# A fused AdaLN block: softmax slots in pairs, a look-ahead of 24 maxima, gating spread over tiles, division by block turns

## What is computed

```
x: (4, 2048, 256);  mod = silu(c) @ wmod -> sa, ca, ga, sb, cb, gb  per batch
h = layernorm(x) * (1 + ca) + sa
x = x + ga * FAVOR_attention(h)          # 16 heads of 16, 64 random features each, linear in T
h = layernorm(x) * (1 + cb) + sb
x = x + gb * FFN(h)
FFN(h): 4 experts, each a quarter (512) of the tokens, h normalised once more,
        expert e uses the first m = 256 >> e channels;
        q, k, v from xn[:, :m];  8 heads of 32 over all 2048 tokens
        attn = softmax(q k^T * scale);  out_e = (attn @ v)[:, :m] @ o_w[:m, :m].T + o_b[:m], + h
```

## Time and profile before

| | |
|---|---|
| Median of 3 runs | 1817.99 us (1814.53 to 1819.95) |
| Profiled execution | 1821.6 us, span 1819.5 us |
| PE busy | 1704.0 us (94%), 11538 products |
| DVE busy | 1397.6 us (77%) |
| ACT, POOL busy | 1101.9 us (61%), 1142.2 us (63%) |
| Maxima: product, reduction | 960 x 447 ns, 960 x 681 ns |
| Scores, exponentials | 960 x 406 ns, 960 x 601 ns |
| Values, denominators | 1920 x 608 ns, 960 x 592 ns (two records to a product) |
| Mean granted clock | 0.975 |

### The profile page before, as it was taken

The page is one execution under the profiler, slowest core; times in us unless marked ns, Lnnn a source line. Parts: engine busy times, 40 slices in busy tenths (PEclk is TensorE's granted clock), DMA queues, the critical chain, the costliest instruction groups (busy, mean ns, idle before and its releaser), DMA issues.

```text
span 1819.5 us, 31846 instructions
## 1 busy us (share of the span) xinstructions
PE 1704.0 (94%) x11538; PEld 973.2 (53%) x11538; DVE 1397.6 (77%) x2621; ACT 1101.9 (61%) x2066; POOL 1142.2 (63%) x1062
## 2 busy tenths in 40 slices
PE   6999999999799989999989998999988999899997
PEld 4775544444477554444357755444436765444443
DVE  5887877777588788777678878777758888777774
ACT  1885536666588544666658844465656875356664
POOL 2784358667678345766768724776685862477666
PEclk8999989999999999999999999999999999899999
DMA  5000350010200045001120005300111001620101
GB/s 182 2 2 1 128 159 10 18 44 4 90 2 2 1 154 133 16 12 45 35 59 2 1 23 180 85 19 10 44 59 36 2 2 50 191 54 11 41 13 47
DMA packets 56076, 89.55 MB, mean 49 GB/s; under 512 B 13288, under 2 KB 31976, under 8 KB 53100
## 3 DMA queue, kind: packets, MB, share of 16 engines
q1 hardware_dynamic: 54768, 87.45, 16.4%
q10 hardware_dynamic: 1152, 0.07, 0.0%
HBM read 49.29 MB, written 35.72 MB: 47 GB/s over the span
## 4 chain that ended last, share of the span: by engine, by line
PE 67%; DVE 13%; ACT 8%; POOL 5%; issue 3%; DMA 2%; SPq 2%; ACTq 0%; POOLq 0%; DVEq 0%
PE PS L1466 14%; PE PS L1651 13%; PE PS L1639 11%; PE PS L1664 6%; PE PS L1364 5%; PE PS L1372 3%; PE PS L1389 3%; PE PS L1399 3%; DVE MXP L1067 3%; ACT HT L639 2%; ACT HTR L642 2%; DVE STAT L960 2%; ACT PR L860 1%; DVE QKS L1136 1%; PE PS L1515 1%
## 5 line engine op out<-in xcount | busy, mean ns | idle before, releaser
L602 POOL TENSOR_TENSOR TS<-PR 128x1024 f32<-128x1024 f32 (+1 forms) x256 | 573.5, 2240 | 300.4 <-ACT PR L860 235.9
L1067 DVE TENSOR_REDUCE MXP<-PS 128x1 f32<-128x512 f32 x960 | 600.5, 681 | 178.3 <-PE PS L1466 177.5
L860 ACT ACTIVATE PR<-PS 128x512 f32<-128x512 f32 x960 | 503.1, 601 | 355.6 <-PE PS L1639 351.0
L1466 PE MATMUL PS<-KOP,QOP 96*128 96x512 f32 x960 | 418.4, 447 | 11.6 <-DVE MXP L1067 5.0
L1639 PE MATMUL PS<-QOP,KOP 97*128 97x512 f32 x960 | 376.9, 406 | 14.8 <-ACT PR L860 11.5
L1466 PEld LDWEIGHTS PS<-KOP,QOP 96*128 96x128 f32 x960 | 184.4, 193 | 277.4 <-DVE MXP L1067 216.2
L1651 PE MATMUL PS<-PR,V 128*32 128x512 f32 x1920 | 275.7, 608 | 0.0
L1639 PEld LDWEIGHTS PS<-QOP,KOP 97*128 97x128 f32 x960 | 180.5, 191 | 77.9 <-ACT PR L860 45.9
L1664 PE MATMUL PS<-TS,ones 128*32 128x512 f32 x960 | 133.1, 592 | 5.5 <-POOL TS L602 5.5
L522 POOL TENSOR_SCALAR PK<-XSK 128x1024 f32<-128x1024 f32 x64 | 67.2, 1050 | 98.4 <-ACT XSK L698 98.1
L1399 PE MATMUL PS<-PB,QKT 64*128 64x256 f32 x1536 | 126.5, 297 | 1.0 <-DVE VE L954 1.0
(11 more groups left out here) (153 smaller groups left out, 2629.1 us busy)
## 6 DMA issues: line engine op xcount, KB each, us to landing
KOP<-k_scr SPq DMA_DIRECT2D x84, 256.0 KB, 5.5
k_scr<-QKS SPq DMA_DIRECT2D x64, 256.0 KB, 2.9
QOP<-q_scr SPq DMA_DIRECT2D x180, 64.0 KB, 2.0
q_scr<-QKS SPq DMA_DIRECT2D x40, 256.0 KB, 3.0
X<-in_L_attn_x_dram SPq DMA_DIRECT2D x16, 512.0 KB, 4.7
out_dram<-X SPq DMA_DIRECT2D x12, 512.0 KB, 3.1
QOP<-MXT SPq DMA_DIRECT2D x224, 0.5 KB
KOP<-QKS SPq DMA_DIRECT2D x36, 64.0 KB, 2.0
```

The costliest lines, as they stand in the source:

```text
L602: g.tensor_tensor(sums(k)[:, 0:len(stage)], pair[:, :, 0], pair[:, :, 1], ALU.add).then_inc(S["psum_t"], 1)
L860: a.activation(PR[:, k % 2, w, q], bank(score_bank(p, n, w, q)), ACT.Exp).then_inc(S["ex"], 1)
L1067: v.tensor_reduce(MXP[:, u % 2, i, kc:kc + 1], bank(max_bank(p)), AX.X, ALU.max).then_inc(S["am_rd"], 1)
L1466: mm(bank(max_bank(p)), QOP[0:96, u % QS6, i * P:(i + 1) * P], KOP[0:96, h % KS6, kc * CH:(kc + 1) * CH], start=True, stop=True).then_inc( ...
```

## The change

- PE: slots 0 to 7 (stage 0) as before, with the values of slot 7 at their end; from slot 8 on slots go in pairs: three times a maximum and a score, five times a score and a maximum, then the denominators of the pair before, then the values of both slots; an output stands behind them.
- `LOOK` is 24: two more maxima stand before slot 0, and the stream ends with pair 26 (slots 52 and 53).
- DVE: eight maxima to a pair; the additions of a finished stage behind the fifth and the eighth maximum of the next stage's first pair. The division of a part is one call: 32x32 block turns of the whole row of `SUM` (512 columns), the reciprocal of one column in 32, a copy that spreads it over 32 columns, and turns back; the buffers lie in rows of `Hh` that are free by then, which the wait on `base` makes sure of.
- ACT: the upper values are copied before the first exponentials of the next stage, the upper sums behind those of its second slot.
- POOL: the gate products are three pieces at tiles 4, 5 and 6 (`GATE` = 4); the bias follows seven tiles behind (`LAG` = 7). DVE's residual waits for the tiles that it reads and not for all.

```diff
@@ -84,7 +84,7 @@
 
-    LOOK = 22
+    LOOK = 24
     stream = [(0, i, kc) for kc in expert for i in range(TPC)]
...
@@ -92,7 +92,7 @@
     PER_P = 17
-    LAG = 4
+    GATE, LAG = 4, 7
     SETUP_BANK = (0, 1, 7, 2, 6, 7, 0, 1)
...
@@ -177,6 +177,9 @@
         Hh = sb("Hh", [P, NT, D])
+
+        TURN = Hh[:, NT - TPC:NT - TPC + 2].rearrange("p t d -> p (t d)")
+        ONE = Hh[:, NT - 1, 0:CH // DH]
 
...
@@ -501,15 +504,15 @@
 
-            def gated_output(b):
-                if b == 0:
+            def gated_output(b, part):
+                if b == 0 and part == 0:
                     wait_all(pool, (S["mod_in"], 16), (S["setup_ok"], 1))
-                gate = MODB[:, bass.ds(b, 1), 0, :]
-                g.tensor_tensor(WoG[:], WoT[:], gate.broadcast_to([P, KD, D]), ALU.mult).then_inc(S["gated"], 1)
-                g.tensor_tensor(BOG[:], BO[:], gate.rearrange("p o d -> p (o d)"), ALU.mult).then_inc(S["gated"], 1)
+                gate = MODB[:, bass.ds(b, 1), 0, :].rearrange("p o d -> p (o d)")
+                dst, src = (BOG[:], BO[:]) if part == KD else (WoG[:, part], WoT[:, part])
+                g.tensor_tensor(dst, src, gate, ALU.mult).then_inc(S["gated"], 1)
 
             def with_bias(b, t):
-                wait_all(pool, (S["gated"], 2 * (b + 1)))
+                wait_all(pool, (S["gated"], (KD + 1) * (b + 1)))
                 g.tensor_tensor(X[:, t], X[:, t], BOG[:], ALU.add).then_inc(S["xb"], 1)
...
@@ -524,8 +527,8 @@
                         low_h(b, t + 2)
-                    if at == LAG:
-                        gated_output(b)
+                    if GATE <= at < GATE + KD + 1:
+                        gated_output(b, at - GATE)
                     if at >= LAG:
...
@@ -607,7 +610,7 @@
                             rows = min(width[z], P)
-                            wait_all(pool, (S["rcp"], TPC * (len(RECIPROCALS) * b + i + 1)))
+                            wait_all(pool, (S["rcp"], len(RECIPROCALS) * b + i + 1))
                             g.tensor_tensor(NUM[0:rows, z], NUM[0:rows, z], SUM[0:rows, z], ALU.mult
...
@@ -833,13 +836,17 @@
 
-                def upper_rows(p):
+                def upper_values(p):
 
...
                     a.activation(CS[0:rows, 0], PS[2 * DH:2 * DH + rows, 6, :], ACT.Copy).then_inc(S["cs_up"], 1)
+
+                def upper_sums(p):
+
+                    rows = acc_rows(p)
                     act.wait_ge(S["den2"], SLOTS // 2 * b + STEPS // 2 * (p + 1))
...
@@ -854,14 +861,17 @@
                         act.wait_ge(S["psum_t"], SLOTS * b + k - 1)
+                    if n == 0 and p > 0:
+                        upper_values(p - 1)
                     for w in range(len(stages[p])):
...
                                          ).then_inc(S["ex"], 1)
-                    if n == 0 and p > 0:
-                        upper_rows(p - 1)
-                upper_rows(len(stages) - 1)
+                    if n == 1 and p > 0:
+                        upper_sums(p - 1)
+                upper_values(len(stages) - 1)
+                upper_sums(len(stages) - 1)
 
...
@@ -1105,8 +1115,7 @@
                     g, two = NC * b + s, slice(s * TPC + 2 * h, s * TPC + 2 * h + 2)
-                    if s == 0 and h == 0:
-                        dve.wait_ge(S["xb"], NT * (b + 1))
+                    dve.wait_ge(S["xb"], NT * b + TPC * s + 2 * h + 2)
                     dve.wait_ge(S["yps"], 2 * g + h + 1)
...
@@ -1201,30 +1210,35 @@
                 maxima(MAXU, LOOK)
-                for k in range(SLOTS):
-                    p0 = LOOK + k * 4
-                    if k % STEPS == 1 and k > STEPS:
-                        p = k // STEPS - 1
-                        maxima(p0, p0 + 1)
+                for m in range(SLOTS // 2):
+                    p0 = LOOK + 8 * m
+                    if m % (STEPS // 2) == 0 and m > 0:
+                        p = 2 * m // STEPS - 1
+                        maxima(p0, p0 + 5)
                         finish(dve, v, b, p, 0)
-                        maxima(p0 + 1, p0 + 2)
+                        maxima(p0 + 5, p0 + 8)
                         finish(dve, v, b, p, 1)
-                        maxima(p0 + 2, p0 + 4)
                     else:
-                        maxima(p0, p0 + 4)
-                    for z, at in RECIPROCALS:
-                        if k in (at, at + 1):
-                            if k == at:
-                                dve.wait_ge(S["c_out"], len(stages) * b + len(stages) - 2)
-                            for q in (2 * (k - at), 2 * (k - at) + 1):
-                                divide_part(z, q).then_inc(S["rcp"], 1)
+                        maxima(p0, p0 + 8)
+                    for i, (z, at) in enumerate(RECIPROCALS):
+                        if 2 * m == at:
+                            dve.wait_ge(S["c_out"], len(stages) * b + len(stages) - 2)
+                            dve.wait_ge(S["base"], 2 * NC * (b + 1))
+                            if i > 0:
+                                dve.wait_ge(S["rcp"], len(RECIPROCALS) * b + i)
+                            sums_divided(z).then_inc(S["rcp"], 1)
                     for i, e in enumerate(results[:-1]):
-                        if k == OUT_SLOTS[e]:
+                        if 2 * m == OUT_SLOTS[e]:
                             result(b, i)
 
-            def divide_part(z, q):
-                part = SUM[0:min(width[z], P) if z < NC else P, z, q * P:(q + 1) * P]
-                return v.reciprocal(part, part)
+            def sums_divided(z):
+
+                rows = min(width[z], P) if z < NC else P
+                own(v.transpose(TURN[0:rows], SUM[0:rows, z]))
+                own(v.reciprocal(ONE[0:rows], TURN[0:rows].rearrange("p (n k) -> p n k", k=DH)[:, :, 0]))
+                own(v.tensor_copy(TURN[0:rows].rearrange("p (n k) -> p n k", k=DH),
+                                  ONE[0:rows].rearrange("p (n o) -> p n o", o=1).broadcast_to([rows, CH // DH, DH])))
+                return v.transpose(SUM[0:rows, z], TURN[0:rows])
 
...
@@ -1261,8 +1275,9 @@
                 dve.wait_ge(S["fin_n"], len(stages) * (b + 1))
+                dve.wait_ge(S["rcp"], len(RECIPROCALS) * (b + 1))
+                own(sums_divided(NC))
                 for q in range(TPC):
-                    own(divide_part(NC, q))
                     part = slice(q * P, (q + 1) * P)
...
@@ -1505,7 +1520,7 @@
                     if s == 0:
-                        pe.wait_ge(S["gated"], 2 * (b + 1))
+                        pe.wait_ge(S["gated"], (KD + 1) * (b + 1))
                         pe.wait_ge(S["phiq"], 2 * NT * (b + 1))
...
@@ -1677,20 +1692,35 @@
                 pe.wait_ge(S["q_lo"], NQ * (b + 1))
-                for k in range(SLOTS):
+                def score_of_pair(m, i):
+
+                    score(2 * m + i // 4, i % 4 // 2, i % 2)
+
+                for k in range(STEPS):
                     p0 = LOOK + 4 * k
...
                         maxima(p0 + i, p0 + i + 1)
-                        if k > 0 and i // 2 < len(stages[k // STEPS]):
-                            score(k, i // 2, i % 2)
+                        if k > 0 and i < 2:
+                            score(k, 0, i)
                     if k >= 1:
...
                         denominators(k // 2 - 1)
+                values(STEPS - 1)
+                for m in range(STEPS // 2, SLOTS // 2):
+                    p0 = LOOK + 8 * m
+                    for i in range(3):
+                        maxima(p0 + i, p0 + i + 1)
+                        score_of_pair(m, i)
+                    for i in range(3, 8):
+                        score_of_pair(m, i)
+                        maxima(p0 + i, p0 + i + 1)
+                    denominators(m - 1)
+                    values(2 * m)
+                    values(2 * m + 1)
                     for i, e in enumerate(results[:-1]):
-                        if k == OUT_SLOTS[e]:
+                        if 2 * m == OUT_SLOTS[e]:
                             output(i)
-                values(SLOTS - 1)
                 denominators(SLOTS // 2 - 1)
...
```

## The result

The kernel with the change takes 1797.18 us (median of five runs, 1795.75 to 1804.53), the one before 1817.8 beside it (1814.53 to 1819.95). The ratio is 0.9894, with a 95% interval of 0.9872 to 0.9915: 1.1% faster, and outside the 0.3% that can't be told from no change. The profiled execution took 1797.2 us, its span 1795.4; the sum in the prediction had 1797.8 for it. Of the medians 1794 was forecast: the change took off 20.6 us where 24 were expected.

What follows compares the result with a forecast made beforehand. PE's matrix work was taken to bound the slot loop. Terms 27.8 - 4.8 + 5.0 + 0.6 - 4.8 = 23.8 us took the profiled 1821.6 to 1797.8, and the median 1818.0 to 1794 us; 8-in-10 range 1780 to 1811.

Steps and rivals of the forecast that it cites:

- The pair: Long slot loop, slots in pairs: 6.99 us a pair becomes 6.87; with stage beginnings and batch end, 27.8 us gained.
- rival of a free pair: Long slot loop: the weights' early load takes up the waits, a pair takes 6.71 us, kernel 1779 us; chance 0.15.
- that of 7.07: Rival in the long slot loop: the rings of three bound, a pair takes 7.07 us, kernel 1812 us; chance 0.14.
- score 4's early ask: Inside a pair: score 4 asks for its bank just as it is freed, putting the next product at 1.84, not 1.745.
- The stage beginnings: Where a stage begins in the slot loop: waits of 0.4 three times and 0.9 twice, 3.0 us a batch, should go.
- The look-ahead: Before the slots: two more maxima in DVE's unbroken run, 1.2 us a batch, a cost of 4.8 us.
- Pairs 27 to 31: Batch end, pairs without maxima: 6.43 us each, 0.98 more with an output; POOL's last sum ends at 7.50.
- Gating: Tiles 4 to 6 on POOL: gating spread and bias lag 7 save 1.26 a batch, 5.0 us.
- Joints: Between batches: POOL waits for the first variance behind output 2, 1.6 us lost each, 4.8 us for three.
- The end: Kernel end: division by block turns saves 0.6 us, once.
- Turn: DVE's division: a block turn of 512 columns taken as 0.70 us; a rival had 3.39, kernel 1835 us, chance 0.05.
- The clock: Rival in front of the slots: middle batches lose the 2 us batch 0 loses, kernel 1798 or 1803 us; chance 0.10.

Runs made afterwards that it cites:

- e1_strict: Changed kernel with maximum and score strictly alternating through all eight of a pair; 1835.8 us, ratio 1.0092 to the kernel before.
- e11_four: Changed kernel with outputs in PE's wait and no division copy (1784.2 us), now four maximum-score then four score-maximum in pairs with maxima; 1784.82 us.
- e2_look22: Changed kernel with a look-ahead of 22 instead of 24, pairs kept; 1814.29 us, ratio 0.9969 to the kernel before.
- e0_after_again: The changed kernel run once more, unchanged; 1804.84 us, its six runs in two heaps, 1795.3 to 1798.9 and 1810.8 to 1811.4.
- e8_output_in_wait: Changed kernel with the outputs of pairs 29 to 31 moved from behind the values to behind score 3; 1797.89 us, ratio 0.9882.
- e7_nocopy: Changed kernel without the division's copy, the second turn reading each reciprocal 32 times; 1809.29 us, ratio 0.9934.

## Why the prediction was right

**The pair (6.87 forecast, 6.85 measured): right, and by its mechanism.** The waits were put where PE's rows show them, the 0.33 to 0.35 that follow a held weight load among them. The rival of a free pair (6.71) is refuted by the weight rows, that of 7.07 is what e1_strict built and measured at 7.05. One detail was too much: e11_four shows that score 4's early ask costs nothing of its own: the pair is as long with that score behind maximum 4. The stage beginnings went: all pairs with maxima read 6.79 to 6.89, but for one of 7.12 in batch 2. The kernel before had six such beginnings a batch, four of 0.4 and two of 0.9, so 3.4 and not 3.0; the sum, worked out from the whole stretch of 201.0, doesn't hang on it. That the stretch from slot 8 on came to 27.6 against 27.8 has luck in it: at full clock the stretch came some 0.4 a batch shorter than forecast, and the lower clock in batch 2 took 1.6.

**The look-ahead: the sum right, the account of it not complete.** The forecast charged 1.2 a batch for two more maxima in front and measured 4.8 in sum, but spread as -0.3, +4.5, -0.3 and +0.9, which is not the uniform charge of the step: that the sums agree is luck, for the 4.5 comes from one short stretch of the kernel before. e2_look22 puts the price of the two maxima at 2.6 a batch on average, from one execution of each. And the step named no gain, though there is one of 4.7 a batch: the end of a unit falls outside the run of maxima at 24 and not at 22. The forecast of 6.87 for *every* pair had silently assumed it. Had the look-ahead been 22, the same working would have missed the pairs by 19 us.

**Pairs 27 to 31: 6.43 and 7.41 forecast, 6.37 and 7.37 to 7.40 measured,** except pair 28. There the prediction hid the copy of the upper values behind the exponential's start at 0.85, which holds only while maxima stand between the scores; without them it is 0.28 later. That is 1.1 us in four batches.

**Gating: 7.25 for 8.56 at tile 4, as forecast.** **Joints: 1.62 for 1.6.** **The end: 1.0 for 0.6.** **Turn: 0.71 for 0.70; reciprocal 0.25 for 0.30.** The copy was read from a copy out of PSUM, 0.69. It is 0.43 alone and up to 5.14 beside POOL, in the same place in three batches of four: the range of this term should have been open upwards, for the trace of before had no copy within SBUF beside POOL's sums. In the change PE had slack for it, in e8_output_in_wait it had not.

**The clock: the rival looked in the wrong place.** It was put in front of the slots. There the granted clock rose from 0.91 to 0.93 and 0.94 in batches 0 and 2, stayed at 0.94 in batch 3 and fell from 0.97 to 0.93 in batch 1 (0.52 from 686 to 693 after; before, 0.76 from 692 to 699). The larger risk was in the last pairs, where the earlier trace rows already showed waits of 0.31 and where no maxima stand in between. In the profiled execution batch 2 paid 1.6 us, in e0_after_again two batches paid 6.9 and two joints 5.4. The eleven executions of the kernel lie between 1795.3 and 1811.4, six of them up to 1799, two at 1802 and 1805, three at 1811; the second median is 1804.8, and the highest runs stand at the edge of the range. That the first five gave 1797.2 is luck in part.

**What stays open.** Why the stretch in front of slot 8 was 3 to 5 us shorter in batch 1 of the kernel before than in its other batches: the wait for operands and the lower clock both lie there, and no run held one of them still. Whether the turns are worth more than their 1.0 at the end of the kernel while the pairs' waits are unfilled. Which of two waiting instructions, DVE's copy or POOL's next, gets in. What decides, in one execution, whether the clock falls in a batch.

## What to carry to other kernels

Where a run of products goes through rings of three banks, write down for each product the reader that frees its bank: one reader's pace sets the run, and the order in which two rings are served decides which (0.49 in the change, 0.60 in e1_strict). Put a reader's other work (the end of a unit, a division) outside that run; a look-ahead that is a multiple of the run does this. And look at PE's short waits not only for their length: here waits of 0.2 to 0.6 us brought the array to half its clock in some executions. Useful work moved into them shortened the pairs and came with the full clock where it stood; in a pair left unfilled the clock could still fall (e11_four).

## What the runs showed of the hardware

A copy of 128x512 within SBUF on DVE takes 0.43 us with POOL idle. Started while POOL was in a product or a sum, it ended about 0.3 behind one of POOL's: behind that product in pair 30 (0.48 long), behind the two sums that followed it in pair 29 (5.14 long). Started 0.08 into POOL's norm of the next batch (L481, at 470.15) it took 0.46, and POOL's instruction took 1.47 where its neighbours take 1.22. The Trainium skill ("SBUF — State Buffer", Who interferes with whom) says that such copies can use two ports, that the second pair is shared with GpSimd, and that one of the two then blocks for the whole instruction. The lengths agree with that; that DVE can stay blocked over two more instructions of POOL in a row, and in another pair gets in between them, the runs add. Nothing here shows what decides it.

A turn of 128x512 takes 0.71 on DVE, from dense columns as from one that is read 32 times (e7_nocopy), where 32 columns took 0.21.

The same program ran its last pairs at 2.4 GHz in one execution and partly at 1.2 GHz in another, 13 us apart in all; six useless products a pair came with 2.4 GHz throughout these pairs in the profiled execution, at no cost (1796.12 us, four runs within 2.7).
